# A transformer block in one kernel, cross-attention stage: half of the second key projection of an odd tile is issued ahead of the transposes of the tile before it

## What is computed

```python
x = x + xattn(layernorm(x), ctx_1024, ctx_1024, Wq, bq, Wk, bk, Wv, bv, Wo, bo)   # 16 heads of 16, softmax over 256 keys
x = x + attn(layernorm(x), w_qkv, b_qkv, w_out, b_out)                            # causal self-attention
x = x + ffn(layernorm(x), w_gate, w_up, w_down)                                   # quantized gated MLP

# cross-attention:
q = (queries @ Wq.T + bq).reshape(B, L, H, E)
k = (keys @ Wk.T + bk).reshape(B, S, H, E)
v = (values @ Wv.T + bv).reshape(B, S, H, E)
scores = jnp.einsum('blhe,bshe->bhls', q, k)
attn = jax.nn.softmax(scores * E ** -0.5, axis=-1)
out = jnp.einsum('bhls,bshe->blhe', attn, v).reshape(B, L, H * E) @ Wo.T + bo
```

## Time and profile before

| | us |
|---|---|
| median of 3 executions | 884.32 (883.75 to 885.76) |
| profiled execution, its own time | 883.71 |
| span of that execution in the trace | 881.7 |
| PE busy | 850.0 (96%) |
| DVE busy | 756.1 (86%) |
| ACT busy | 693.2 (79%) |
| POOL busy | 482.8 (55%) |

### The profile page before, as it was taken

One profiled execution on the slowest core, in us unless ns is written; L12 is line 12 of the kernel. 1 busy time (PEld: TensorE's weight loads), 2 busy tenths in 40 slices (PEclk: granted clock), 3 DMA queues, 4 the chain that ended last, 5 costly groups with the idle time before them and its releaser, 6 DMA issues.

```text
span 881.7 us, 28587 instructions
## 1 busy us (share of the span) xinstructions
PE 850.0 (96%) x9750; PEld 714.4 (81%) x9750; DVE 756.1 (86%) x1583; ACT 693.2 (79%) x2045; POOL 482.8 (55%) x710
## 2 busy tenths in 40 slices
PE   7999999999999999999999988999999998999997
PEld 6889888898888888988888867888888875666664
DVE  6888888888888888888888877999999988999995
ACT  4778887777777777787777765888888877999996
POOL 4433234355554555334433327878787864777775
PEclk9999999999999999999999998999999999999999
DMA  4351110111011111111111000000000000000011
GB/s 135 116 175 50 48 42 30 50 44 48 30 42 48 38 46 35 42 48 33 39 48 36 13 2 1 2 3 1 0 1 0 1 3 1 31 31 30 30 36 36
DMA packets 31635, 31.84 MB, mean 36 GB/s; under 512 B 3280, under 2 KB 30800, under 8 KB 31568
## 3 DMA queue, kind: packets, MB, share of 16 engines
q1 hardware_dynamic: 30448, 30.47, 11.0%
q10 hardware_dynamic: 1120, 0.59, 0.2%
HBM read 26.86 MB, written 4.19 MB: 35 GB/s over the span
## 4 chain that ended last, share of the span: by engine, by line
PE 78%; ACT 12%; issue 5%; DVE 2%; POOL 2%; DMA 0%; DVEq 0%; ACTq 0%; POOLq 0%; SPq 0%
PE psum L353 12%; PE psum L310 9%; PE psum L324 9%; PE psum L340 8%; PE psum L380 7%; PE psum L688 5%; ACT probs L1063 4%; PE psum L726 3%; PE psum L737 3%; PE psum L389 3%; PE psum L364 3%; ACT probs L520 3%; PE psum L297 2%; PE psum L780 2%; PE psum L707 2%
## 5 line engine op out<-in xcount | busy, mean ns | idle before, releaser
L520 ACT ACTIVATE probs<-psum,nmax 128x256 f32<-128x256 f32 x512 | 235.6, 487 | 57.0 <-DVE nmax L477 56.8
L551 POOL TENSOR_TENSOR rm<-rinv,hm_sb 128x256 f32<-128x256 f32 x64 | 39.7, 620 | 260.6 <-DVE rinv L449 260.6
L477 DVE TENSOR_REDUCE nmax<-psum 128x2 f32<-128x512 f32 x256 | 159.0, 684 | 11.6 <-PE psum L340 11.4
L353 PE MATMUL psum<-id_sb,probs 128*128 128x128 f32 x1024 | 126.4, 275 | 0.9
L353 PEld LDWEIGHTS psum<-id_sb,probs 128*128 128x128 f32 x1024 | 114.3, 141 | 4.3 <-ACT probs L520 4.2
L520 ACT ACTIVATION_READ_ACCUMULATOR probs<-psum,nmax 128x1 f32 x512 | 112.3, 219 | 0.0
L544 POOL TENSOR_TENSOR cl<-c_sb,ch 128x512 fp32r<-128x512 f32 x64 | 81.8, 1278 | 10.0 <-ACT ch L495 9.2
L340 PE MATMUL psum<-k_sb,qb 32*128 32x256 f32 x1024 | 75.1, 401 | 2.3 <-DVE qb L433 1.2
L528 POOL TENSOR_TENSOR rstd<-vare,minus_half 128x1 f32<-128x1 f32 x96 | 53.4, 556 | 36.3 <-DVE vare L410 32.5
L340 PEld LDWEIGHTS psum<-k_sb,qb 32*128 32x128 f32 x1024 | 47.0, 184 | 21.3 <-issue 17.8
L899 POOL TENSOR_TENSOR w_all<-c_sb,qm_sb 128x1024 f32<-128x1024 f32 x32 | 60.6, 1895 | 3.1 <-ACT c_sb L844 3.1
(11 more groups left out here) (162 smaller groups left out, 2502.6 us busy)
## 6 DMA issues: line engine op xcount, KB each, us to landing
c_sb<-in_ctx_t SPq DMA_DIRECT2D x64, 256.0 KB, 2.8
x_sb<-in_x SPq DMA_DIRECT2D x32, 128.0 KB, 2.5
out<-y_sb SPq DMA_DIRECT2D x32, 128.0 KB, 1.7
w_all<-in_w_gate SPq DMA_DIRECT2D x1, 1024.0 KB, 5.1
w_all<-in_w_up SPq DMA_DIRECT2D x1, 1024.0 KB, 6.6
w_all<-in_w_down SPq DMA_DIRECT2D x1, 1024.0 KB, 6.4
wqkv_sb<-in_w_qkv SPq DMA_DIRECT2D x1, 768.0 KB, 6.9
wk_sb<-in_wk ACTq DMA_DIRECT2D x1, 256.0 KB, 4.1
```

The costliest lines, as they stand in the source:

```text
L353: last = nc.tensor.transpose(sp[g][:, c:c + P], probs[:, 2 * g + u, kh * P:(kh + 1) * P], id_sb[:])
L477: nc.vector.tensor_reduce(nmax[:, 2 * g:2 * g + 2], sp[g].rearrange("p (u s) -> p u s", u=2), AX.X, ALU.max, negate=True).then_inc(max_don ...
L520: nc.scalar.activation(probs[:, j, :], sp[g][:, u * S:(u + 1) * S], ACT.Exp, bias=nmax[:, j:j + 1], accum_out=rsum[:, j:j + 1]).then_inc(e ...
```

## The change

`pe_k` can now issue one of its halves: its waits go with half 0, its signal `k_mm` with half 1. In even tiles from 2 on, half 0 of the keys (t + 1, 1) is issued behind the values (t + 1, 0) and ahead of T(t, 1). The odd tile behind it, tile 31 included, begins with half 1 alone. Tile 1, whose forerunner is tile 0, still begins with both.

```diff
-        def pe_k(pe, t, s):
+        def pe_k(pe, t, s, halves=(0, 1)):
+
             b = t * 2 + s
-            pe.wait_ge(ch_done, b + 1)
-            pe.wait_ge(cl_done, b + 1)
-            pe.wait_ge(k_ev, b)
-            for m in range(KT):
+            if 0 in halves:
+                pe.wait_ge(ch_done, b + 1)
+                pe.wait_ge(cl_done, b + 1)
+                pe.wait_ge(k_ev, b)
+            for m in halves:
...
-            last.then_inc(k_mm, 1)
+            if 1 in halves:
+                last.then_inc(k_mm, 1)
...
-                def body(t, n, j, first=False, wsum=False, ahead2=True):
-
-                    pe_k(pe, t, 1)
+                def body(t, n, j, first=False, second=False, wsum=False, ahead2=True):
+
+
+                    pe_k(pe, t, 1, (1,) if j and not second else (0, 1))
                     pe_v(pe, t, 1)
...
                     if wsum:
                         pe_wsum(pe, t)
+                    if j == 0 and not first:
+                        pe_k(pe, t + 1, 1, (0,))
                     pe_transpose(pe, t, 1)
...
-                body(1, 0, 1)
+                body(1, 0, 1, second=True)
...
-                pe_k(pe, t, 1)
+                pe_k(pe, t, 1, (1,))
```

## The result

The changed kernel takes 885.70 us (883.93 to 887.37, 22 runs), against 884.25 us (882.50 to 887.02, 22 runs) of the kernel before in the same session: a ratio of 1.0017, 95% interval 1.0011 to 1.0024. It is 1.5 us slower. That is under the 0.2% at which a difference was to count, but the interval is clear of 1. Its profiled execution took 885.87 us, with a span of 883.9 us.

The account below looks back on a forecast made before the run. PE was taken to bound the cross-attention stage, its waits for ACT's exponentials (4.2 us) being the whole prize. Terms -4.1 + 3.0 + 0.5 = -0.6 us gave 883.7 us; own range 882.5 to 885.1, whole range 882.3 to 886.6.

Parts of the forecast that it names:

- rival 3: Odd tile's first transposes wait for late exponentials, making the kernel slower: 2.1 us in all, 886.4 us; chance 0.17.
- Removed wait: Even tiles' second transposes: all 14 waits of PE's loads for ACT's exponentials go, -4.1 us.
- Added wait: Moved half in even tiles waits for DVE's k_sb: 0.20 us a pair, bounds 0 and 0.29, +3.0 us.
- Where the chain to k_sb starts: DVE reaches k_sb from the output projection over y, values and four maxima, 4.02 us; filling PE doesn't shorten it.
- What is late next: Scores, maxima and exponentials come 0.65 us later; odd tile's first transposes lose 0.03 us a pair, +0.5 us.
- Any other wait in the odd tile: Sign of a wrong prediction: the +0.65 us delay reached further than it was followed.
- The sum: Whole kernel: -4.1 + 3.0 + 0.5 = -0.6 us, forecast 883.7 us.
- The rule of the weight loads: Skill says PE pulls loads ahead of matmuls in flight; if past the added wait, it costs 0.11 us, not 0.20.
- Rival 1: Half's first weights are loaded ahead of the added wait: 1.3 us less, 882.4 us; chance 0.14.
- Rival 2: Keys ready in time at the half, odd tile's spare time suffices: all 4.1 us won, 880.2 us; chance 0.09.

Follow-up runs that it names:

- e1: The change, with the moved half's waits for ch_done and cl_done put ahead of the values (t + 1, 0), k_ev alone at the half: 884.83 us, ratio 1.0005.
- e8: The change, with DVE's move of the values (t, 1) ahead of y (t - 1) instead of behind it: 885.98 us, ratio 1.0015.
- e9: The change, with DVE's k_sb ahead of the fourth maximum in even tiles instead of behind it: 881.74 us, ratio 0.9970.
- e7: The change, but only four matmuls of the half moved, between groups 2 and 3 of the even tile's second transposes: 880.44 us, ratio 0.9961.
- e4: The change, but only two matmuls of the half moved, between groups 2 and 3 of the even tile's second transposes: 880.81 us, ratio 0.9962.
- e3: The change, but the half's six matmuls between groups 2 and 3 of the even tile's second transposes: 881.58 us, ratio 0.9968.

## Why the prediction was wrong

The time, 885.7 us, lay in the whole range of 882.3 to 886.6 us, but outside the forecast's own of 882.5 to 885.1. The forecast was 0.6 us faster with no measurable difference, and the kernel is 1.5 us slower, clear of noise. It came out as rival 3 on its sign, though its size lies under the 0.2% that I had asked of it, and only in small part by rival 3's mechanism: the odd tiles' first transposes did wait, but most of the loss came from elsewhere. By steps:

- **Removed wait: right.** The 14 waits, 4.1 us, are gone; the even transposes take 1.84 us.
- **Added wait: the step that failed, by its size.** It was to cost 0.20 us a pair and cost 0.29, just the upper bound. That is 15 x 0.09 = 1.4 us of the 2.1 us between forecast and result. k_sb ended 0.06 us behind the time at which the half was due, in the change (252.54 and 252.48) as in the earlier trace rows (251.47 and 251.41), and the restart was 0.08 us: both as taken. What I had too small was the release. I took 0.05 us, from a row of a load that one DVE result had released (the row itself gives 0.06); here it was 0.12, since this matmul waits for three semaphores (e1: 0.06 with one). And the matmul came 0.03 us behind its load, a term that the prediction did not have. 0.06 + 0.12 + 0.03 + 0.08 = 0.29 us.
- **Where the chain to k_sb starts: incomplete in the reading, right in the consequence.** It hangs on the scores too, not on the output projection alone (e8). Filling PE shortens neither, so the half was late in all even pairs as forecast; but who believes the first reading looks for the remedy in the wrong place, as I did.
- **What is late next: right for the transposes of tile 15, not for all, and missed for the scores.** I had the last group's load 0.07 us late and took 0.03 us for it; in tile 15 it was 0.02 to 0.03. But one pair stood for all fifteen: five odd tiles lose 0.07, and tile 31, where PE comes to the transposes 0.2 us sooner still, 0.3 us. I followed the exponentials to the transposes and stopped there. ACT's copies behind them are late by the same amount, and the second scores wait 0.05 us for the last of them: 15 x 0.05 = 0.8 us more. That is the second step that failed, a term that I had put at nothing. "Any other wait in the odd tile" was named as what would prove me wrong, and this is it. The prediction wrote that the values, y, q and the second transposes were untouched, and never mentioned these scores.
- **The sum.** -4.1 + 15 x (0.29 + 0.03 + 0.05) = +1.5 us, which is what was measured. The fit is somewhat lucky: it takes tiles 14 and 15 for all, and leaves out tile 31's 0.3 us. With that it is 1.8 us; the interval of the ratio, 1.0 to 2.1 us, holds both.
- **The rule of the weight loads.** Rival 1 had the first weights of the half loaded during the wait. The Trainium skill, page TensorE: Matmul & The Clock Gate, section "Step-by-step: what each phase is for", has loads pulled ahead of matmuls in flight. In mid-stream the trace shows them 0.10 us ahead; at this wait load and matmul begin 0.03 us apart, at 252.66 and 252.69, and in e1 at one time, so the pull-ahead does not reach past a wait for a semaphore here, which is what the prediction's sum had assumed.
- **Rival 2** needed k_sb 0.2 us sooner. e9 made it so, and that gained 2.4 us, not the 4.1 us I had priced: the odd tile keeps its loss, by the table 0.09 us a pair or 1.3 us, and the wait in tile 31 is there too (0.33 us). The interval of e9's ratio (1.3 to 3.9 us) holds the rest.

## What to carry to other kernels

Work that is moved into a wait brings its own conditions along: before it is moved, ask when the buffer that it overwrites is free, to a tenth of a microsecond, and place it where that is long so. Here 0.26 us were to be won, and the same six matmuls lose 1.5 us in front of the transposes and win 2.1 to 2.3 us behind their second or third group. And what fills one tile is taken from another: fill the wait, and stay under what the other tile has to spare (two matmuls, 0.24 us, left 0.05 of the wait of 0.26; four, 0.47 us, left 0.01 and cost the odd tile nothing; six, 0.71 us against 0.65 to spare, cost it 0.07 us and more in some tiles). Look at the odd ones out among the tiles, too, before one pair is taken for all; and follow the delay through every consumer of what comes late, the copies too, not only to the first one that has slack.

## What the runs showed of the hardware

- A matmul that waits for three semaphores, the last one given by DVE, started its load 0.12 us behind the end of DVE's instruction; with one semaphore to wait for, 0.06 us (the change and e1, all 14 waits of each). The trace files the first kind under "issue", so such a group of idle loads can hide a wait for another engine.
- A wait held on the path cost the matmul stream its lateness and 0.08 us more: the first three pairs behind it took 0.79 us instead of 0.71, the same as the keys behind r. With the wait gone and all else on PE the same (e9) they took 0.71.
- The releaser that the trace names can be the wrong one of two: DVE was named for the scores' wait, and moving DVE's copy 0.7 us ahead took the name away and left the wait; ACT's copy was the late one. In e7 the name stands at 14 waits that cost nothing.
- Runs of one kernel differ by more than the change does, and the granted clock of the whole run goes with it. Of the 35 runs of the kernel before that e1 to e4 stand against, the 11 at 0.997 or 0.998 took 882.26 to 882.96 us, the 10 at 0.996 883.65 to 884.54, the 6 at 0.992 885.23 to 887.23. At 0.996, e3's ten runs took 881.17 to 882.21 us, so its gain is not the clock's.
